# Two input stages: sequences enter in pairs at even distances instead of in fours

## The reference, cut to what matters

```python
# layer 0 mixer, on h = layernorm(x)
x_n = h * time_mix_n + shift(h) * (1 - time_mix_n)      # n = r, k, v, g
r = sigmoid(x_r @ W_r.T + b_r); g = silu(x_g @ W_g.T + b_g)
k, v = l2norm_per_head(x_k @ W_k.T + b_k), l2norm_per_head(x_v @ W_v.T + b_v)
# layer 1 mixer, on h = layernorm(x)
xn = h * rsqrt(mean(h * h) + 1e-6) * norm_w
xc, z = split(xn @ in_proj_w.T)                          # 512 channels each
xc = silu(causal_conv_4(xc) + conv_b); zs = silu(z)
dt = softplus(xc @ dt_w.T + dt_b) + 1e-4; dx = dt * xc; B, C = xc @ B_w.T, xc @ C_w.T
```

## Time and profile before

| | |
|---|---|
| median of three runs | 8376.84 us |
| the profiled execution | 8381.71 us, span 8379.6 us |
| VectorE busy over the span | 6666.1 us (80%) |
| TensorE busy | 6244.1 us (75%) |
| ScalarE busy | 3461.7 us (41%) |
| GpSimd busy | 3671.7 us (44%) |
| mean granted clock of TensorE | 0.910 |

### The profile page before, as it was taken

How to read it: one execution, slowest core, us unless ns; L and a number is a source line. 1 busy time by engine, 2 the same in 40 slices (tenths; PEclk the granted TensorE clock), 3 DMA queues, 4 the chain that set the end, 5 groups by cost and what they waited for, 6 DMA issues and landing times. The chain is left out here.

```text
span 8379.6 us, 122772 instructions
## 1 busy us (share of the span) xinstructions
PE 6244.1 (75%) x40740; PEld 4178.7 (50%) x40740; DVE 6666.1 (80%) x11381; ACT 3461.7 (41%) x6666; POOL 3671.7 (44%) x1911
## 2 busy tenths in 40 slices
PE   5455554888866677777777777777677769999999
PEld 3355554677755322222222222222244448888888
DVE  6799997555567899999999999999744547676765
ACT  3333332333323566666666566666444321212121
POOL 0000000111100599999999999999611112222222
PEclk8777776999988899999999999999888879999999
DMA  2211112111022100000000000000011110000000
GB/s 63 72 42 42 42 44 61 39 36 36 19 78 108 63 14 15 15 14 15 15 14 21 19 17 14 15 15 8 29 41 36 36 66 7 8 7 8 7 8 6
DMA packets 335677, 254.47 MB, mean 30 GB/s; under 512 B 161763, under 2 KB 307046, under 8 KB 334854
## 3 DMA queue, kind: packets, MB, share of 16 engines
q1 hardware_dynamic: 332774, 248.29, 9.5%
q10 hardware_dynamic: 2464, 0.26, 0.0%
HBM read 140.46 MB, written 108.00 MB: 30 GB/s over the span
## 5 line engine op out<-in xcount | busy, mean ns | idle before, releaser
L1809 POOL TENSOR_TENSOR ss_inp<-ss_dx,ss_b_all 128x1024 f32<-128x1024 f32 x1024 | 2390.2, 2359 | 230.1 <-ACT ss_b_all L1783 227.9
L1827 DVE TENSOR_TENSOR_SCAN ss_h<-banks,ss_inp 128x1024 f32<-128x1024 f32 x1024 | 2313.0, 2278 | 59.9 <-ACT banks L1775 59.9
L1747 PE MATMUL banks<-ss_ch,ident 128*128 128x512 f32 x4096 | 1959.5, 601 | 64.9 <-DVE ss_xc L1843 64.9
L1775 ACT ACTIVATE banks<-ss_dt,ss_neg_a 128x510 f32<-128x510 f32 x2048 | 1334.7, 688 | 2.7 <-DVE ss_h L1827 2.7
L1725 PE MATMUL banks<-ss_bc,ss_pick 96*128 96x512 bf16 x2048 | 747.0, 386 | 787.8 <-DVE ss_ch L1836 750.2
L1783 ACT COPY ss_b_all<-banks 128x512 f32<-128x512 f32 x1024 | 600.4, 586 | 1235.7 <-PE banks L1725 1232.0
L1747 PEld LDWEIGHTS banks<-ss_ch,ident 128*128 128x128 f32 x4096 | 788.0, 193 | 635.9 <-issue 577.9
L1725 PEld LDWEIGHTS banks<-ss_bc,ss_pick 96*128 (+1 forms) x2048 | 200.0, 98 | 1662.7 <-issue 1484.6
L1836 DVE TENSOR_TENSOR ss_ch<-ss_h,banks 128x1024 f32<-128x1024 f32 x768 | 917.9, 1195 | 0.0
L605 PE MATMUL banks<-ms_rprod,ident 128*128 128x128 f32 x2048 | 466.8, 400 | 507.9 <-DVE ms_rprod L691 507.9
L2139 POOL TENSOR_TENSOR pk_blockhot<-pk_onehot,pk_parts 128x2048 bf16<-128x2048 bf16 x96 | 345.5, 3628 | 1099.7 <-DVE pk_parts L2377 1099.7
(11 more groups left out here) (293 smaller groups left out, 10344.9 us busy)
## 6 DMA issues: line engine op xcount, KB each, us to landing
keep_v<-ms_cx_values SPq DMA_DIRECT2D x32, 512.0 KB, 2.8
l_va<-keep_v SPq DMA_DIRECT2D x32, 512.0 KB, 5.3
l_kf<-keep_k SPq DMA_DIRECT2D x32, 256.0 KB, 4.1
keep_x<-l_x SPq DMA_DIRECT2D x32, 256.0 KB, 2.2
keep_xc<-si_xc SPq DMA_DIRECT2D x16, 512.0 KB, 3.0
keep_zs<-si_zs SPq DMA_DIRECT2D x16, 512.0 KB, 4.0
keep_dt<-si_acc SPq DMA_DIRECT2D x16, 512.0 KB, 2.6
keep_dx<-si_acc SPq DMA_DIRECT2D x16, 512.0 KB, 2.6
```

The lines of the kernel that those rows point to most:

```text
L1747: m = T_.matmul(sums[j][:, :], chip.ident[:, :], ch[u][:, j, :], start=first, stop=False, skip_group_check=True)
L1775: last = A.activation(decay[u % 2][:, j, :, 1:T], inputs[i % 2][0][:, j, :, 1:T], ACT.Exp, scale=neg_a[:, i % 2 * HB + j, bass.ds(k * UN + ...
L1809: G_.tensor_tensor(inp[u][:, :, :], inputs[i % 2][1][:, :, :, :].rearrange("p j g t -> p j (g t)"), rep(b_all[u][:, :], 1, HB), ALU.mult). ...
L1827: V.tensor_tensor_scan(flat(h[u][:, :, :]), decay[u % 2].rearrange("p j g t -> p (j g t)"), flat(inp[u][:, :, :]), 0.0, ALU.mult, ALU.add) ...
```

## The change

Both stages get new starts. Sequences enter in pairs, one round apart, a pair each 12 rounds in A and each 20 in B; a slot is used again after 24 and 40 rounds, as before. SyncE's generator is split in two: `load`, which starts eight rounds before its sequence (not below round 0), and `store`, which starts at round 22 of its sequence in A, and with it in B. In B, ScalarE issues Ln in the same step as Exp; no round of other sequences' instructions lies between them.

```diff
-    def sync(S, b, z, i):
+    def load(S, b, z, i):
         if i:
             S.wait_ge(*z.norm.normed.at(i - 1))
         S.dma_start(z.x[:, :, :], rows(io["x"][b])).then_inc(z.x_loaded.sem, DMA)
-        for _ in range(22):
-            yield
+        yield
+
+    def store(S, b, z, i):
         S.wait_ge(*z.scaled.at(i))
...
+    def starts(later=0):
+
+        return [max(0, PACE * (b // 2) + b % 2 + later) for b in range(B)]
+
+    def each(program, engine):
+        return [program(engine, b, st.slots[b % 4], b // 4) for b in range(B)]
+
     def all_of(program, engine):
-        rounds([program(engine, b, st.slots[b % 4], b // 4) for b in range(B)], [SPAN * (b // 4) + b % 4 for b in range(B)])
-
-    SPAN = 24
+        rounds(each(program, engine), starts())
+
+    PACE, AHEAD, STORE = 12, 8, 22
...
-    all_of(sync, nc.sync)
+    rounds(each(load, nc.sync) + each(store, nc.sync), starts(-AHEAD) + starts(STORE))
...
-    def sync(S, b, z, i):
+    def load(S, b, z, i):
         if i:
             S.wait_ge(*z.x_stored.at(i - 1))
         S.dma_start(z.x[:, :, :], rows(dr["x1"][b])).then_inc(z.x_loaded.sem, DMA)
+        yield
+
+    def store(S, b, z, i):
         yield from nothing(7)
...
         A.activation(flat(z.dx), flat(z.dx), ACT.Exp).then_inc(z.exp_done.sem, 1)
-        yield
         A.wait_ge(*z.exp_done.at(i))
         A.activation(flat(z.dx), flat(z.dx), ACT.Ln, bias=1.0).then_inc(z.softened.sem, 1)
+        yield
         yield
...
-    S, SPAN = nc.sync, 40
+    S, PACE, AHEAD = nc.sync, 20, 8
...
-    all_of(sync, nc.sync)
+    rounds(each(load, S) + each(store, S), starts(-AHEAD) + starts())
```

## The result

The change makes the kernel slower: 8442.1 us (median, 8440.6 to 8445.2) against 8376.6 us (8373.8 to 8382.4), a ratio of 1.0077 with a 95% interval of 1.0064 to 1.0089. The forecast was 8454 us, slower, with a range of 8345 to 8500.

A forecast was written before the change was run, and what follows sets the result against it. Stages add up between barriers; in A and B VectorE is busiest, idling for projections and token loads. Profiled 8381.7 + 57.5 (A) + 19.4 (B) - 4.9 (profiled run over median) = 8454 us, range 8345 to 8500.

The forecast's parts named there:

- A, first half: Stage A (mixer_inputs), steps 0 to 10 of the first pair, before the whole periods: 22.8 us.
- A, last half: Stage A, end after seven whole periods: 24 us with the clock up, 27.7 with two slow projections.
- B, last half: Stage B (ssm_inputs), last convolutions, eight projections and the closing chain after the whole periods: 34.3 us.
- Loads: Both stages: loads queued eight rounds ahead remove VectorE's whole load wait, 78 us, but the projection is late next.
- Pairs in A, the trips: Stage A: VectorE waits 10.4 us per two-sequence period for projection round trips; period 34.2 us, stage +2.0, clock up.
- The clock in A: Stage A: idle gaps drop TensorE's clock, four of eight projections slow, 7.4 us a period; stage +57.5 us.
- Pairs in B: Stage B: TensorE paces part of each period, 8.7 us idle plus 1.8 slow restart; period 53.0, stage +19.4 us.
- Exp and Ln: Stage B: adjacent Exp and Ln form a 10.3 us chain for a pair; VectorE waits 2.4 at b's add.
- The clock holds: Rival: evenly spread projections keep TensorE's clock up; +2.0 in A, +5.8 in B, 8385 us; chance 0.14.
- The trips are covered: Rival: pairs drift, half the projection waits disappear under the other pair's work, clock up; 8318 us; chance 0.16.
- Colder: Rival: all eight projections of each period of stage A slow; A +115 us, total 8511 us; chance 0.07.
- One table load for Exp and Ln: Rival, stage B: both chains 1.28 us shorter and the 2.4 wait goes, 17 off: 8437 us; chance 0.06.

The follow-up runs named there:

- experiment 2: Kernel before with only the loads issued eight rounds ahead in both stages, sequences still in fours and Ln a round after Exp: 8305.1 us, ratio 0.9916.
- experiment 3: Changed kernel with unread transposes added on TensorE in all four long idle stretches of each period of stage A: 8388.2 us, ratio 1.0014.
- experiment 4: Changed kernel with Ln put back one round after Exp in stage B: 8462.6 us, ratio 1.0104.
- experiment 5: Changed kernel with unread transposes only in the two longest idle stretches of each period of stage A, the two of 2.2 us left: 8397.2 us, ratio 1.0028.
- experiment 1: Stage A as in the changed kernel, stage B as in the kernel before: 8434.3 us, ratio 1.0070.

## Why the prediction was right

It held in sign, size and mechanism; 8454 us was 12 us above the median. Some of that closeness is luck. By the profiled executions the change cost 59.2 us where the forecast had 76.9, 17.7 too many; the medians lie 65.5 us apart, and so 6 us of the error don't show. Term by term (us, from the profiled executions):

| term | forecast | measured |
|---|---|---|
| A, first half | 22.8 | 20.6 |
| A, whole periods | 7 x 41.6 = 291.2 | 7 x 41.4 = 290.0 |
| A, last half | 27.7 | 24.0 |
| A, whole stage | +57.5 | +50.4 |
| B, first half | 24.5 | 23.3 |
| B, whole periods | 7 x 53.0 = 371.0 | 7 x 51.4 = 359.8 |
| B, last half | 34.3 | 38.2 |
| B, whole stage | +19.4 | +10.9 |
| other stages | 0 | -2 |

*Loads.* Forecast as gone, and as late next the projection. Both are seen; experiment 2 adds that without the pairs the whole of it would have been kept.

*Pairs in A, the trips.* The queue written out gave 23.8 us of work and 10.4 of uncovered trips, 34.2 us. Experiment 3 shows this period by itself, with the clock up: 34.20. Its eight waits, in the forecast's order from 1b on, are 2.09, 1.29, 1.93, 1.44, 0.35, 0.85, 1.58 and 0.95 us, each within 0.2 of the forecast; they sum to 10.5, because the 0.5 us set down for the copy of b did not come and most of the others were a little longer. Writing out the instructions that stand between a mix and its bias was what carried this. The stage with the clock up came to 282.2 us against 286.2 forecast; the halves were a little too large.

*The clock in A.* Forecast: idle stretches of 4.0, 3.3, 2.35 and 2.35 us; measured 3.99, 3.08, 2.22 and 2.22. Forecast: four of eight projections wholly slow, 4 x 1.85 = 7.4 us a period. Measured: five partly slow, with 1.66 + 1.63 + 1.02 + 1.51 + 1.07 = 6.9 us over 1.99. So the count was one too low and the price too high, because each is slow for a part of its length only, and the two nearly cancel. That it is a cost and not a symptom is shown by experiment 3: 52.4 us for the stage, against 57.5 - 2.0 = 55.5 forecast. The halves are most of A's error of 7.1 us: I charged the first with a slow second projection (it took 1.99) and the last with two of 3.78, where all took 1.99.

*Pairs in B.* The period was 1.6 us too long in the forecast. For the projections, the pads and the slow restart I had 8.7 + 1.8 = 10.5 us of idleness, and the stretch shown has 51.87 - 39.76 - 2.56 = 9.6. The first half was forecast 1.2 too long and the last 3.9 too short: -11.2 - 1.2 + 3.9 = -8.5 us, B's whole error. The slow restart is there: in that period TensorE had been idle for 14.10 us when its transposes began, the clock read 0.50 from 2510 to 2515 us, and the first projection (start 2512.35) took 3.44 us. What the clock costs B as a whole (forecast 19.4 - 5.8 = 13.6 us) no experiment parts from the rest.

*Exp and Ln.* The chain was forecast at 10.3 us from a's Exp to the end of b's Ln, and is 10.3; the wait at b's add was forecast at 2.4, and is 2.56 in the period shown, 19.8 over nine such waits. What I had not worked out is what the adjacency saves when pairs are given: 18 us (experiment 4). I had counted only what it leaves.

*Rivals.* The clock holds: wrong, though experiment 3, with the clock up in A, came near what it would have been: 8388 us, forecast 8385. The parts agree less well than the sum: A came 2.0 us below the kernel before (forecast 2.0 above), B, where nothing was filled, 10.5 above (forecast 5.8). The trips are covered: wrong, all 64 projections are waited for. Colder: wrong, three of eight stay at 1.99. One table load for Exp and Ln: wrong. Ln's loads in B (line, engine, operation, count, busy us, mean ns, idle before) are still 16, as in the earlier trace rows:

```profile
L1583 ACT ACT_TABLE_LOAD x16 | 20.5, 1283 | 0.3
```

The Trainium skill, page "ScalarE: Activation LUTs", section "Table sets: the hidden batching unit", has one set with both functions and so one load for the two. Neither trace agrees, not even with the two instructions adjacent: 16 loads for 16 Ln, 1283 ns each.

## What to carry to other kernels

Before splitting a group of interleaved work items to spread it more evenly, write out the bound engine's queue for one period and count what stands between each producer and its consumer: with four items in step VectorE waited 50.1 us in A for a round trip of 2 us, with two in step and the clock up 89.0, and the stage was 41.8 us longer, although VectorE's work was unchanged. Moving a load ahead of the stores that wait is a separate edit with a separate gain (70 us here); try it by itself. And where a matmul engine is half busy, look at how its idle time is cut up: the same projections, single and with idle stretches of 2.2 to 4.0 us between them, ran at the lower clock just where another engine waited (37 of 64, 52.6 us).

## What the runs showed of the hardware that was not expected

- Unread transposes made a stage faster: 56 more of them on TensorE in a period took 6.8 us off its length (41.0 to 34.2), with the granted clock at 1.00 throughout.
- An idle stretch of 2.22 us on TensorE was followed by a slow projection in every regular period of the changed kernel and in the first periods of experiment 5, but not in the later periods of experiment 5, where the stretches were as long and the queue the same. The instructions ahead of it were the same too. I can show the two behaviours but not what chooses between them.
- The slow projection behind the same stretch grew from period to period in the changed kernel: 2.92, 3.01, 3.08, 3.12, 3.15 us (starts 39.89 to 203.97, each about 41 us after the last). In the next projections the pattern broke (six projections of over 3 us in that period, which took 44.1 us), and it began again at 2.89. So the slow part moved against the kernel's own period, although the idle stretches in it stayed the same; what it follows is not shown. Two kernels with the same stage can differ by a few us in it (4.3 in experiment 1).
- In the period shown the clock read 1.00 from 98 to 102 us, where TensorE was idle but for 0.28 us, and 0.56 from 102 to 104, around its restart: the price fell on the first projection behind the stretch, which has a consumer waiting, and not on the idleness.
